# A post-norm layer with routed experts on one core: rows of maxima placed by TensorE and copied by ScalarE instead of transferred, and a new order of SyncE's list

## What is computed

```python
q, k = rope(x @ wq + bq), rope(x @ wk + bk)
v = x @ wv + bv
attn = softmax(q @ k.T / sqrt(8) + causal)
x = layernorm(x + (attn @ v) @ wo + bo)
idx = argmax(softmax(x @ wg)); gate = its probability, 0 where the expert is full
x = layernorm(x + gate * (x @ W[idx].T + b[idx]))
```

## Time and profile before

| | |
|---|---|
| median of 3 runs | 418.27 us (418.15 to 418.33) |
| profiled execution | 417.29 us |
| its span, first to last instruction | 415.5 us |
| TensorE busy | 340.7 us, 82% |
| VectorE busy | 326.3 us, 79% |
| GpSimd busy | 285.5 us, 69% |
| ScalarE busy | 269.9 us, 65% |
| packets of SyncE's DMA queue | 58.9% of 16 engines' span |
| packets of ScalarE's DMA queue | 3.0% |

### The profile page before, as it was taken

The page is one execution under the profiler, slowest core; times in us unless marked ns, Lnnn a source line. Parts: engine busy times, 40 slices in busy tenths (PEclk is TensorE's granted clock), DMA queues, the critical chain, the costliest instruction groups (busy, mean ns, idle before and its releaser), DMA issues.

```text
span 415.5 us, 11631 instructions
## 1 busy us (share of the span) xinstructions
PE 340.7 (82%) x4230; PEld 279.9 (67%) x4230; DVE 326.3 (79%) x871; ACT 269.9 (65%) x633; POOL 285.5 (69%) x508
## 2 busy tenths in 40 slices
PE   4445596989989988898899989998999896987781
PEld 4334384868777877787777868786878785866561
DVE  5678664768989997999898989998989985875454
ACT  5252385758677866868595859695968585778500
POOL 6273337376688877787778787888879785575543
PEclk9968587999999999999999999999999999999976
DMA  5297948686968586857767676768586869310000
GB/s 153 76 174 143 144 114 127 106 147 117 143 120 160 108 141 132 163 100 148 138 134 132 138 136 126 146 118 167 110 162 113 157 112 165 24 43 2 16 13 25
DMA packets 150727, 48.76 MB, mean 117 GB/s; under 512 B 113311, under 2 KB 146979, under 8 KB 150670
## 3 DMA queue, kind: packets, MB, share of 16 engines
q1 hardware_dynamic: 144766, 43.70, 58.9%
q10 hardware_dynamic: 5184, 2.36, 3.0%
q0 software_dynamic: 720, 1.97, 1.5%
HBM read 28.60 MB, written 14.68 MB: 104 GB/s over the span
## 4 chain that ended last, share of the span: by engine, by line
PE 39%; DVE 14%; DMA 13%; ACT 13%; SPq 8%; issue 7%; POOL 2%; ACTq 2%; DVEq 0%; POOLq 0%
DMA q_plain<-max_rows 7%; DMA q_diag<-plain_parts 6%; PE ps_m L1051 4%; PE ps_ab L1137 4%; PE ps_ab L1121 4%; PE ps_pv L1152 4%; ACT high L693 3%; PE ps_m L1053 3%; PE ps_m L1052 3%; PE ps_ab L1105 3%; ACT ps_ab L697 3%; SPq L445 3%; SPq L489 3%; DVE row_max L911 2%; DVE low L901 2%
## 5 line engine op out<-in xcount | busy, mean ns | idle before, releaser
L693 ACT ACTIVATE high<-ps_ab 128x448 f16<-128x448 f32 (+1 forms) x192 | 100.9, 525 | 41.6 <-PE ps_ab L1121 40.9
L911 DVE TENSOR_REDUCE row_max<-ps_ab 128x2 f32<-128x512 f32 (+3 forms) x176 | 109.5, 628 | 12.7 <-PE ps_ab L1137 12.4
L540 POOL TENSOR_TENSOR low<-probs,high 128x384 f16<-128x384 f32 (+1 forms) x64 | 64.4, 1016 | 13.0 <-ACT probs L697 11.7
L901 DVE TENSOR_TENSOR low<-ps_ab,high 128x448 f16<-128x448 f32 (+1 forms) x80 | 47.1, 589 | 28.3 <-ACT ps_ab L697 28.3
L697 ACT ACTIVATE ps_ab<-ps_ab 128x448 f32<-128x448 f32 (+1 forms) x128 | 67.7, 529 | 0.0
L1121 PE MATMUL ps_ab<-q_plain,k_diag 128*128 128x128 bf16 (+1 forms) x768 | 66.5, 214 | 0.0
L1137 PE MATMUL ps_ab<-k_plain,q_diag 128*128 128x192 bf16 (+3 forms) x512 | 66.1, 243 | 0.0
L1152 PE MATMUL ps_pv<-v_mov,high 128*128 128x64 bf16 x768 | 64.6, 194 | 0.9 <-ACT low L701 0.7
L1152 PE MATMUL ps_pv<-v_mov,low 128*128 128x64 bf16 x768 | 64.4, 193 | 0.0
L1099 PE MATMUL ps_ab<-mask_a_bf,ident_bf 128*128 128x128 bf16 (+2 forms) x176 | 45.3, 257 | 19.5 <-DMA q_diag<-plain_parts 12.6
L1105 PE MATMUL ps_ab<-mask_b_bf,ident_bf 128*128 128x128 bf16 (+1 forms) x192 | 47.5, 247 | 15.2 <-DMA q_plain<-max_rows 6.1
(11 more groups left out here) (188 smaller groups left out, 928.5 us busy)
## 6 DMA issues: line engine op xcount, KB each, us to landing
plain_parts<-rot SPq DMA_DIRECT2D x180, 64.0 KB, 2.2
k_plain<-plain_parts SPq DMA_DIRECT2D x16, 384.0 KB, 4.2
q_diag<-plain_parts SPq DMA_DIRECT2D x32, 192.0 KB, 5.6
q_plain<-plain_parts SPq DMA_DIRECT2D x16, 384.0 KB, 4.8
k_diag<-plain_parts SPq DMA_DIRECT2D x32, 192.0 KB, 4.2
v_mov<-v_parts SPq DMA_DIRECT2D x64, 48.0 KB, 2.0
x_in<-in_L_attn_x_dram SPq DMA_DIRECT2D x16, 128.0 KB, 5.4
out_dram<-y_out POOLq DMA_DIRECT2D x15, 128.0 KB, 2.5
```

The lines of the kernel that those rows point to most:

```text
L540: pool.tensor_tensor(fine(low, k), kept_probs(k), fine(high, k), ALU.subtract).then_inc(s_["low_pool"], 1)
L693: act.activation(fine(high, k), b_scores(k), ACT.Exp, scale=SCALE)
L901: dve.tensor_tensor(fine(low, k), b_scores(k), fine(high, k), ALU.subtract)\
L911: last = dve.tensor_reduce(row_max[:, NBLK - 1 - j, groups[0]:groups[-1] + 1], scores[:, :, col:col + width(j)], AX.X, ALU.max)
```

## The change

- `max_parts` becomes one row of 96 + 4 x 48 columns, with 96 columns of zeros ahead (they stay zero). For each of 4 blocks of tokens and 2 halves of the heads, `ex` takes 120 columns of it as the stationary operand, such that the 24 wanted columns come last. The output has 120 rows, and the maxima stand in rows 96 to 119 of PSUM, the rows in which q_plain wants them. That is 8 matmuls of 64 moving columns in place of 2.
- ScalarE copies rows 96 to 119 straight into q_plain, with two activations that read each half four times over (`broadcast_to`). The tile max_rows, the two DMAs and the semaphore maxrows_loaded go; the first b chunk waits for maxrows_done. The copies wait for the end of the second pass of sequence b - 2 (`b_ready`), the last reader of that q_plain.
- SyncE's list: q_plain moves from ahead of rot_1's writes to behind them, with its wait on `b_ready`; the second half of k_diag moves from ahead of rot_3's writes to behind them; v moves from ahead of k_plain and q_diag to behind them. The first sequence's v stands there already.
- The tables of slots stay as they are.

```diff
-        max_parts = sb("max_parts", [128, NBLK, 64], bf)
-        max_rows = sb("max_rows", [2 * MAX_ROWS, S], bf)
+        max_parts = sb("max_parts", [128, SCORE_ROWS + NBLK * 2 * MAX_ROWS], bf)
...
-                if b_ahead:
-                    after(sp, "b_ready", b - 2, NB, NB)
-                    load_q_plain(b, p)
-
...
                 if not (is_step(s, -1) or is_step(s, 0)):
                     write(rot_1, 0, "rot1_done")
                 if b_ahead:
+                    after(sp, "b_ready", b - 2, NB, NB)
+                    load_q_plain(b, p)
                     load_k_diag(b, p, 0)
                 write(rot_2, 1, "rot2_done")
+                write(rot_3, 2, "rot3_done")
                 if b_ahead:
                     load_k_diag(b, p, 1)
-                write(rot_3, 2, "rot3_done")
-                if has(b) and not is_step(s, 0):
-                    load_v(b, p)
                 if has(a):
                     after(sp, "parts_written", a, PARTS_WRITTEN, PARTS_WRITTEN)
...
-                if is_step(s, 0):
+                if has(b):
                     load_v(b, p)
...
                         after(act, "ex_ready", b, 1, 1)
-                        after(act, "maxrows_loaded", b, 2 * 16)
-                        for jj in range(2):
-                            last = act.activation(max_rows[:, :].rearrange("m (i jj r) -> m jj i r", i=2, jj=2)[:, jj],
-                                                  ps_n[64 * jj:64 * jj + 2 * MAX_ROWS, 0:2 * BLK]
-                                                  .rearrange("m (i r) -> m i r", i=2), ACT.Copy)
+                        after(act, "b_ready", b - 2, NB, NB)
+                        for half_at in range(2):
+                            last = act.activation(q_plain[pb_][SCORE_ROWS:ONE_ROW, 4 * half_at:4 * half_at + 4, :],
+                                                  ps_n[SCORE_ROWS:ONE_ROW, S * half_at:S * half_at + S].unsqueeze(1)
+                                                  .broadcast_to([MAX_ROWS, 4, S]), ACT.Copy)
                         last.then_inc(s_["maxrows_done"], 1)
-                        after(act, "maxrows_done", b, 1, 1)
-                        after(act, "pv_ready", b - 2, NB, NB)
-                        for half_at in range(2):
-                            act.dma_start(q_plain[pb_][SCORE_ROWS:SCORE_ROWS + MAX_ROWS, 4 * half_at:4 * half_at + 4, :],
-                                          max_rows[MAX_ROWS * half_at:MAX_ROWS * half_at + MAX_ROWS, :].unsqueeze(1)
-                                          .broadcast_to([MAX_ROWS, 4, S])).then_inc(s_["maxrows_loaded"], 16)
...
-                            after(pe, "maxrows_loaded", c, 2 * 16, 2 * 16)
+                            after(pe, "maxrows_done", c, 1, 1)
...
-                        for i in range(NBLK // 2):
-                            mm = pe.matmul(ps_n[:, BLK * i:BLK * i + BLK],
-                                           max_parts[:, 2 * i:2 * i + 2, :].rearrange("p i m -> p (i m)"), stacked_bf[:, :],
-                                           start=(i == 0), stop=True, skip_group_check=True)
+                        for half_at in range(2):
+                            for j in range(NBLK):
+                                at, to = MAX_ROWS * (2 * j + half_at), S * half_at + BLK * j
+                                mm = pe.matmul(ps_n[0:ONE_ROW, to:to + BLK], max_parts[:, at:at + ONE_ROW], stacked_bf[:, :],
+                                               start=(half_at == 0 and j == 0), stop=True, skip_group_check=True)
```

More of the change, by code:

```diff
@@ L262, in layer_kernel @@
         names += """w_loaded vw_loaded ident_loaded late_loaded tables_loaded x_loaded parts_written
-                    aops_loaded0 aops_loaded1 bops_loaded0 bops_loaded1 maxrows_loaded v_loaded
+                    aops_loaded0 aops_loaded1 bops_loaded0 bops_loaded1  v_loaded
                     one_loaded stored""".split()
@@ L320, in max_part @@
         def max_part(i):
-            return max_parts[:, :, 0:2 * MAX_ROWS].rearrange("p j (half t m) -> p j half t m", half=2, t=3)[:, :, :, i, :]
+            return max_parts[:, SCORE_ROWS:].rearrange("p (j half t m) -> p j half t m", j=NBLK, half=2, t=3)[:, :, :, i, :]
         def by_half(t):
@@ L542, in _ @@
             pool.memset(minus_half[:, :], -0.5)
-            pool.memset(max_parts[:, :, :], 0.0)
+            pool.memset(max_parts[:, :], 0.0)
             pool.memset(words(q_diag[0][:, :, :, :, :].rearrange("p g j h r -> p (g j h r)")), 0.0)
```

## The result

| | before | after |
|---|---|---|
| median, us | 418.21 (417.81 to 418.33, 4 runs) | 403.02 (402.82 to 403.57, 4 runs) |
| ratio | | 0.9641 (0.9624 to 0.9657) |
| profiled execution, us (its span) | 417.29 (415.5) | 402.82 (401.0) |
| TensorE busy, us | 340.7 | 337.4 |
| ScalarE busy, us | 269.9 | 292.0 |

The forecast was 416.7 us with a range down to 409.5. The direction was right and the size was not: 14.5 us came off the profiled execution where the sum had 1.6.

What follows compares the result with a forecast made beforehand. TensorE's serial list plus waits for q_diag and the maxima bound the kernel. Terms -6.1 (maxima), -6.0 (q_diag) and +10.5 (eight matmuls) sum to -1.6 us: 415.7 profiled, 416.7 on the runs' scale, range 409.5 to 420.5.

Steps and rivals of the forecast that it cites:

- The balance: TensorE's step: whatever is added at `ex` lengthens it, whatever comes off the waits at L1099 and L1105 shortens it.
- the draw: ScalarE: two longer copies of 2.08 us replace copies and DMA issues of 2.33, so rot_1 begins 0.25 us sooner.
- 21.77 us for TensorE's own list: Middle step after the change: 21.07 us without waits plus 0.70 for the added matmuls at `ex`.
- The eight loads, +10.5 us: TensorE at `ex`: eight matmuls for two at 0.10 us each cost 0.70 us in fifteen sequences; ends 2.7 and 11.
- The step without waits, 21.07 us: Middle steps before: the mean of 21.80 us less 0.74 a step of waits for q_diag and the maxima.
- SyncE's list, 0.75 us: q_diag lands 0.75 us sooner: k_plain issued 1.4 sooner, less 0.65 for k_diag's half in flight.
- the other leg: From an a chunk to a later rot_1: 21.5 us before, 22.0 after; it alternates with the leg from rot_1.
- 1.75 us of waits for q_diag: At the start, ahead of L1099: about this much of the third sequence's 1.9 us wait goes.
- the last wait of 2.57 us: Ahead of L1099 near the end: the last wait for q_diag loses only 0.75 us.
- signs: No L1105 wait for maxima, copies of about 1.04 us, rot_1 right behind, k_plain waiting for plain_parts, among others.
- Short loads: Rival, TensorE at `ex`: 120 columns load like 128, the eight cost 0.18 us a sequence; 410.4 us, chance 0.25.
- The queueing rival: Ahead of L1099: q_plain and k_diag loads queue up, q_diag lands 1.0 us later; 421.5 us, chance 0.14.

Runs made afterwards that it cites:

- e3: Changed kernel with the stationary operands of `ex` 128 columns wide in place of 120: 399.93 us, again 398.86 us, ratio to before 0.96.
- e13: Changed kernel with eight more matmuls with 64-column operands ahead of `ex`, their output written over: 407.6 us in a single run.
- e6: Changed kernel with only v's four loads back ahead of k_plain and q_diag: 413.12 us, ratio to before 0.995.
- e8: Changed kernel with q_plain's load and its wait back ahead of rot_1's writes: 400.05 us, ratio to before 0.9624.
- e8_q_again: Second trial of the changed kernel with q_plain's load and its wait back ahead of rot_1's writes: 401.13 us.
- e9: Changed kernel with v and three unread loads ahead of k_plain in the step of the last q_diag alone: median 7.35 us longer.
- e10: Kernel before with v's loads alone moved behind k_plain and q_diag: 411.81 us, ratio to before 0.987.
- e14: Kernel before with SyncE's new list, but q_plain's load again ahead of rot_1's writes: 413.13 us, ratio to before 0.9921.
- e4: Kernel before with v behind q_diag in one step alone, that of the last q_diag: ratio to before 0.9951.

## Why the prediction was wrong in size

**The balance was the right frame.** The step is TensorE's own list plus the waits for two transfers; both waits went in the middle, the eight matmuls came on top, and ScalarE's change is the draw that it was taken for (1.93 us of copies, taken as 2.08). For the middle the sum has 21.77 us for TensorE's own list after; it takes 21.16. The terms that failed:

*The eight loads, +10.5 us: twice too large.* I took 0.70 us, 0.10 for a load, by counting columns. Measured: 0.33 us, 0.055 for a load; over fifteen sequences 5.0 us, so 5.5 us of the error. The loads of the earlier trace rows give a better estimate when bytes are counted: from 8 four-byte columns (32 bytes, 83 ns) to 128 (512 bytes, 198 ns) is 0.24 ns a byte. 120 two-byte columns are 240 bytes: 133 ns, measured 134; 64 are 128 bytes: 106, measured 112. By the pace of the earlier trace rows, 0.11 us for 512 bytes, 240 bytes are 0.052, measured 0.055, and 128 bytes 0.028, measured 0.035. That the price goes by bytes is a line through four widths, not a mechanism shown: the two-byte loads alone give 0.39 ns a column, (134 - 112)/56, so a price by columns with a rate of its own for each type fits as well. The step from 120 to 128 columns, 134 to 98 ns, is another thing: there the short form sets in. The Trainium skill, "TensorE: Matmul & The Clock Gate", section "Weight-path perf modes — Fast Weight Load (FWL) and DoubleRow", ties it to 128 weights; e3 and e13 agree. What the prediction made of that page's P/1.2 ns, 0.7 us for the eight, was 0.33.

*The step without waits, 21.07 us: 20.90.* I took the waits shown off the mean step. The step from `ex` of the fifth sequence to that of the sixth has neither wait and takes 20.90 us; the one after it shows a wait of 1.36 us at L1099 and one of 0.42 at L1105, 1.78 together, and takes 22.86, 1.96 more. From PE's timeline of before:

```profile
132.33 0.23 PE L1161 MATMUL ps_n<-stacked_bf,max_parts 128*128 128x64 bf16 x2
...
153.23 0.23 PE L1161 MATMUL ps_n<-stacked_bf,max_parts 128*128 128x64 bf16 x2
...
156.79 0.23 PE L1099 MATMUL ps_ab<-mask_a_bf,ident_bf 128*128 128x128 bf16 x1 [1.36 <-DMA q_diag<-plain_parts]
...
159.39 0.27 PE L1105 MATMUL ps_ab<-mask_b_bf,ident_bf 128*128 128x256 bf16 x1 [0.42 <-DMA q_plain<-max_rows]
...
176.10 0.23 PE L1161 MATMUL ps_n<-stacked_bf,max_parts 128*128 128x64 bf16 x2
```

The profile counts a wait from the modelled end of the matmul ahead, not from when the next would have started. With 0.07 us that the a chunks took less in after, it is 0.24 us a step, 2.6 us in eleven.

*SyncE's list, 0.75 us: 1.1, with all three parts off.* v's move gives 1.9 us, not 1.3: where it stands ahead of k_plain in e6 it holds the list for 3.17 us (209.91 to 213.08), not 2.6 + 0.1; less the landing that becomes bare, 21.3/16 = 1.33, that is 1.84. q_plain's costs 1.5, not 0.5: its entry holds the list 0.63 us, near what I took. The wait on `b_ready`, which I called long met, is not (5.6 us in 12 sequences stand at L418), but it lies inside the time of the issue: the half of k_diag behind it takes 0.59 us as well and stands at no wait. What I put at nothing is the landing of the writes issued behind q_plain, which k_plain waits for: 2.97 us after the last issue, where e8 has 2.33. k_diag's gives 1.03 at the issue and costs 0.38 at the landing, where I had 0.6 and 0.65. What mattered more was the other leg, from a first a chunk to rot_1 two sequences on: I took one value, 21.5 us; before has 22.17 on average (it is the longer one where a wait at L1105 lies in it), and after 21.36. The two legs of after make 41.6 us, 20.8 a step, well under TensorE's 21.16, so the waits went as I said, with more to spare.

*At the start, 1.75 us of waits for q_diag should have gone.* None did (6.5 and 6.6 us), so that this stretch came out near its forecast (-2.9 for -2.6) is luck. The 2.9 us are the two waits at L1105 (1.5) and, as far as the trace tells, less of the lower clock: in the two steps from the first `ex` to the third the mean granted clock is 0.72 and 0.86 before, 0.78 and 0.92 after. That was not tried by itself, and the start differs from trace to trace: the second one of after reaches the third `ex` at 83.67 us, and the third sequence's wait for q_diag is nothing in both traces of e3 and 2.7 us in e8_q_again.

**What the sum lacked: the clock at the end.** It gave the last wait of 2.57 us as 0.75 saved. Behind it before ran at 0.66 (350 to 355 us); e9 shows that a long wait there costs 1.25 us more than itself. And from the last first b chunk to the end 2.94 us came off, where the change has nothing but the clock of the last expert matmuls. These differ from execution to execution: this stretch takes 38.44 us in one trace of e8 and 39.81 in the other, 41.37 in before and in e6. It is no property of the change alone, and why the lower level comes there is open. With before at 415 to 417 us on the chips of the experiments, up to 3 us of the first comparison's 15 may belong to it.

Together: -1.6 - 5.5 - 2.6 - 1.3 - 2.9 = -13.9 of -14.5 us. It is no closer than a microsecond or two: the 1.75 us at the start that did not come and the 0.6 us of waits left in the middle stand against the higher clock at the start.

**The rivals.** Short loads was nearest, at 410.4 us, with the wrong reason: 120 columns don't load like 128. The queueing rival had its place right, though not in this kernel: in e6 the waits at the first a chunk are back and 11 us are lost, but what queues there is v's issues. Of the two loads that the rival named, q_plain's among the rot writes costs 1.5 us of lead and k_diag's service 0.38. By the Trainium skill's rule on ring order ("DMA: Bandwidth & Descriptors", section "Queues, rings and completion order") the half of k_diag ahead of it should delay q_diag; it does, and by less than the 1.03 us that its place saves. Of what I listed as signs, the vanished wait at L1105, the copies, rot_1 right behind them and k_plain's waits (21.3 us in 16 sequences) came as told.

## What to carry to other kernels

A wait on an issuing engine's list is paid by everything behind it: read how long each entry holds the list, its wait included, and move what is not urgent behind what is; a large load moved ahead of a small one can also cost at the landing, as q_plain's did. Where two transfers take turns as the last to arrive, one that comes sooner hands part of its gain to the other, as in e10 and e14. Estimate a load of stationary operands by its bytes from the nearest rows, and pad to 128 two-byte columns where that is free; take the pace of a step from a step without waits, not from the mean less the waits shown.

## What was not expected of the hardware

- A load of 120 two-byte columns takes 134 ns, of 64 columns 112, of 128 columns 98: eight more columns are cheaper, 0.18 us a step here.
- Four loads of 128 bytes hold SyncE nearly as long as v's four of 48 KB each: 2.46 us against 2.59.
- After TensorE had waited 4.7 us for q_diag, the granted clock was at the lower level for 2.7 us in which it was always busy (0.78 over 345 to 350 us), and 1.00 behind them; the chunks after the wait took 1.25 us longer. Behind the waits of 2.57 us in before and 2.64 in e6 it fell too; where the wait was 1.38 us (e4) or 0.8 (after) it stayed at 1.00.
- The load of q_plain, moved ahead of six writes of other data, made the last of them land 0.6 us later after its issue (2.97 us, 2.33 in e8).
